# A Mamba layer in two directions: B and C rows, dt and dtx copied together, and dtx made by GpSimd

## The reference, cut to what matters

```python
x = silu(causal_conv(x) + conv_b)                # 256 channels
dt = softplus(x_dbl[..., :64] @ Wdt.T + bdt);  B, C = the 16 + 16 other columns of x @ Wx.T
dA = exp(dt[..., None] * A);  dBx = (dt * x)[..., None] * B[:, :, None, :]
h = dA_t * h + dBx_t;   y_t = sum over 16 states of h * C_t
y = (y + x * Dp) * silu(z);  out = y @ W_out.T
beta = mean(|weight|)                            # of the feed-forward part
w_q = clip(round(weight / (beta + 1e-5)), -1, 1)
```

## Time and profile before

| | |
|---|---|
| median of 3 runs | 1043.89 us (1042.23 to 1044.09) |
| profiled execution | 1041.62 us, span 1039.8 us |
| VectorE (DVE) busy | 906.6 us, 87% |
| GpSimd (POOL) busy | 856.6 us, 82% |
| ScalarE (ACT) busy | 598.6 us, 58% |
| TensorE (PE) busy | 669.3 us, 64% |
| DMA queue q1 | 108.97 MB, 38.1% of 16 engines |

### The profile page before, as it was taken

How to read it: one execution, slowest core, us unless ns; L and a number is a source line. 1 busy time by engine, 2 the same in 40 slices (tenths; PEclk the granted TensorE clock), 3 DMA queues, 4 the chain that set the end, 5 groups by cost and what they waited for, 6 DMA issues and landing times. The chain is left out here.

```text
span 1039.8 us, 9415 instructions
## 1 busy us (share of the span) xinstructions
PE 669.3 (64%) x2124; PEld 221.2 (21%) x2124; DVE 906.6 (87%) x1004; ACT 598.6 (58%) x974; POOL 856.6 (82%) x384
## 2 busy tenths in 40 slices
PE   6537637777667666677567666778576676556432
PEld 3212102222212212122112121213121221012122
DVE  2268769999999999999999999999999999999936
ACT  3436544756476665665476766665575756554414
POOL 0169579999798999999799999997998999997602
PEclk9858867788888788788789889688779788666656
DMA  2344404444343424443453424443433424441002
GB/s 57 99 129 127 143 22 118 140 110 137 95 130 94 130 83 127 133 124 114 114 142 82 137 74 134 127 129 109 120 99 97 142 75 135 124 133 49 0 1 81
DMA packets 84071, 109.56 MB, mean 105 GB/s; under 512 B 21040, under 2 KB 34352, under 8 KB 84016
## 3 DMA queue, kind: packets, MB, share of 16 engines
q1 hardware_dynamic: 84016, 108.97, 38.1%
HBM read 38.65 MB, written 3.15 MB: 40 GB/s over the span
## 5 line engine op out<-in xcount | busy, mean ns | idle before, releaser
L440 POOL TENSOR_TENSOR dbx<-dtx_rep,b_rep 128x1024 f32<-128x1024 f32 x256 | 612.6, 2417 | 63.7 <-DMA dtx_rep<-dtx 45.6
L629 ACT ACTIVATE da_ps<-dt_rep,neg_a 128x512 f32<-128x512 f32 x512 | 350.4, 688 | 339.2 <-DVE hs L892 335.1
L892 DVE TENSOR_TENSOR_SCAN hs<-da_ps,dbx 128x512 f32<-128x512 f32 x256 | 296.9, 1207 | 46.2 <-POOL dbx L440 19.8
L892 DVE TENSOR_TENSOR_SCAN hs<-da_ps,carry,dbx 128x512 f32<-128x512 f32 x256 | 312.2, 1267 | 26.8 <-issue 14.3
L1142 PE MATMUL y_ps<-ch,stack 128*32 128x512 f32 x1024 | 178.4, 775 | 209.7 <-DVE ch L782 135.5
L450 POOL TENSOR_TENSOR ch<-hs,c_rep 128x1024 f32<-128x1024 f32 x96 | 226.1, 2356 | 28.6 <-issue 13.9
L782 DVE TENSOR_TENSOR ch<-hs,c_ps 128x1024 f32<-128x1024 f32 x160 | 191.4, 1196 | 0.0
L1133 PE MATMUL c_ps<-x_dbl,select 128*128 128x512 f32 x256 | 179.5, 789 | 0.0
L1085 PE MATMUL pre<-h_t,w_conv 128*128 128x512 f32 x256 | 120.5, 614 | 7.6 <-ACT xs L530 6.4
L1142 PEld LDWEIGHTS y_ps<-ch,stack 128*32 128x32 f32 x1024 | 24.8, 120 | 324.2 <-issue 220.2
L1133 PEld LDWEIGHTS c_ps<-x_dbl,select 128*128 128x128 f32 x256 | 47.0, 229 | 146.2 <-issue 133.8
(11 more groups left out here) (125 smaller groups left out, 507.7 us busy)
## 6 DMA issues: line engine op xcount, KB each, us to landing
dt_rep<-dt SPq DMA_DIRECT2D x512, 64.0 KB, 2.1
dtx_rep<-dtx SPq DMA_DIRECT2D x512, 64.0 KB, 2.6
b_rep<-bc_rows SPq DMA_DIRECT2D x64, 256.0 KB
c_rep<-bc_rows SPq DMA_DIRECT2D x64, 256.0 KB
h_in<-in_L_attn_hidden_states SPq DMA_DIRECT2D x4, 512.0 KB, 5.6
h_res<-in_L_attn_hidden_states SPq DMA_DIRECT2D x4, 512.0 KB, 6.7
out<-hs SPq DMA_DIRECT2D x4, 512.0 KB, 2.9
bc_rows<-x_dbl SPq DMA_DIRECT2D x16, 64.0 KB, 4.7
```

Source lines behind the costliest of these rows:

```text
L440: nc.gpsimd.tensor_tensor(dbx[:, n % RING], dtx_rep[:, r], b_rep[:, k, :].unsqueeze(1).to_broadcast([P, 2, CHUNK]), ALU.mult).then_inc(dbx ...
L629: nc.scalar.activation(da_ps[:, half % DA_BANKS, :], dt_rep[:, r, e, :], ACT.Exp, scale=neg_a[:, half_of(unit), 2 * (unit % 2) + e, g, k:k ...
L892: nc.vector.tensor_tensor_scan(in_scan_order(hs[:, n % RING, e, :], s), in_scan_order(da_ps[:, (2 * n + e) % DA_BANKS, :], s), in_scan_ord ...
```

## The change

1. dt and dtx become the two halves of one tile `step`, so that one set of 8 copies of 128 KB a slot (`load_step`) replaces `load_dt` and `load_dtx`. Likewise B and C rows lie side by side in HBM and in `bc_rep`, and one load of 512 KB a quad (`load_bc`) replaces `load_b` and `load_c`. Each new load waits for all that either of the old ones waited for.
2. SP's order changes. For the next group: slots 0 and 1, then quads 0, 1 and 2. At a group's start: slots 2 and 3 and quad 3 of the current group.
3. dtx is made by GpSimd (`times_step`), at step 6 instead of 7.
4. GpSimd gives up one C product in kinds 1 and 3 (units 1, 4, 8, 11, 13 instead of 1, 3, 6, 8, 11, 13); VectorE makes it.
5. `w_raw` is loaded early, VectorE sums it right after its first weight copy (line 733), and GpSimd's all-reduce runs before the loop.

```diff
-LATER_STAGES = {"copy x_dbl": 0, "u0": 1, "u1": 2, "take u0": 2, "take u1": 4, "softplus": 5, "dtx": 7}
+LATER_STAGES = {"copy x_dbl": 0, "u0": 1, "u1": 2, "take u0": 2, "take u1": 4, "softplus": 5, "dtx": 6}
...
-POOL_C = ((1, 3, 6, 8, 11, 13),) * NG
+POOL_C = ((1, 3, 6, 8, 11, 13), (1, 4, 8, 11, 13)) * (NG // 2)
...
-        dt = sb("dt", [P, DT, CHUNK])
-        dtx = sb("dtx", [P, DT, CHUNK])
+        step = sb("step", [P, DT, 2, CHUNK])
+        dt, dtx = step[:, :, 0, :], step[:, :, 1, :]
...
+        step_rep = sb("step_rep", [P, 2 * DT, 2, 2, CHUNK])
+        dt_rep, dtx_rep = step_rep[:, :, :, 0, :], step_rep[:, :, :, 1, :]
+        bc_rep = sb("bc_rep", [P, STATES // QUAD, 2, CHUNK])
+        b_rep, c_rep = bc_rep[:, :, 0, :], bc_rep[:, :, 1, :]
...
-        bc_rows = nc.dram_tensor("bc_rows", (NG, 2 * STATES, CHUNK), f32).ap()
+        bc_rows = nc.dram_tensor("bc_rows", (NG, STATES, 2, CHUNK), f32).ap()
...
             load_conv(FWD, conv_in)
+            sp.dma_start(w_raw[:], w_ffn).then_inc(w_raw_in, 16)
...
-                sp.dma_start(bc_rows[s], x_dbl[0:2 * STATES, s % 2, :]).then_inc(rows_stored, 16)
+                sp.dma_start(bc_rows[s].rearrange("n c t -> c n t"), x_dbl[0:2 * STATES, s % 2, :]).then_inc(rows_stored, 16)
+
+            def load_step(b, s, r):
 
                 group = NG * b + s
                 sp.wait_ge(dtx_ready, group + 1)
                 if group:
+                    sp.wait_ge(da_ready, 2 * (UNITS * (group - 1) + last_of_slot(r) + 1))
                     sp.wait_ge(dbx_ready, UNITS * (group - 1) + last_of_slot(r) + 1)
                 for e in range(2):
                     k = BLOCK * (2 * (r % 2) + e)
                     for i in range(QUAD):
+                        sp.dma_start(step_rep[BLOCK * i:BLOCK * (i + 1), r, e], step[k:k + BLOCK, r // 2]).then_inc(step_in[r], 16)
+
+            def load_bc(b, s, k):
 
                 group = NG * b + s
                 sp.wait_ge(rows_stored, 16 * (group + 1))
                 if group:
                     sp.wait_ge(dbx_ready, UNITS * (group - 1) + last_of_quad(k) + 1)
                     sp.wait_ge(ch_pool, pool_c(*before(b, s), last_of_quad(k) + 1))
+                rows = bc_rows[s, QUAD * k:QUAD * (k + 1)].rearrange("n c t -> n (c t)")
+                sp.dma_start(bc_rep[:, k].rearrange("p c t -> p (c t)"),
+                             rows.unsqueeze(1).to_broadcast([QUAD, BLOCK, 2 * CHUNK])).then_inc(bc_in[k], 16)
...
                     if group:
-                        load_dt(b, s, 2)
-                        load_dt(b, s, 3)
-                        load_c(b, s, 3)
+                        load_step(b, s, 2)
+                        load_step(b, s, 3)
+                        load_bc(b, s, 3)
...
                     store_rows(*nxt)
-                    load_dt(*nxt, 0)
-                    load_dt(*nxt, 1)
-                    load_b(*nxt, 0)
-                    load_dtx(*nxt, 0)
-                    load_dtx(*nxt, 1)
-                    load_b(*nxt, 1)
-                    load_c(*nxt, 0)
-                    load_b(*nxt, 2)
-                    load_dtx(*nxt, 2)
-                    load_dtx(*nxt, 3)
-                    load_c(*nxt, 1)
-                    load_b(*nxt, 3)
-                    load_c(*nxt, 2)
+                    load_step(*nxt, 0)
+                    load_step(*nxt, 1)
+                    for k in range(STATES // QUAD - 1):
+                        load_bc(*nxt, k)
 
             store_rows(0, 0)
+            load_bc(0, 0, 0)
+            load_step(0, 0, 0)
+            load_step(0, 0, 1)
             for k in range(1, STATES // QUAD):
+                load_bc(0, 0, k)
             for r in (2, 3):
+                load_step(0, 0, r)
...
+            def times_step(b, s):
+
+                q = NG * b + s
+                pool.wait_ge(dt_ready, q + 1)
+                pool.wait_ge(xs_ready, q + 1)
+                if q:
+                    for k in range(2 * DT):
+                        pool.wait_ge(step_in[k], 2 * QUAD * 16 * q)
+                nc.gpsimd.tensor_tensor(dtx, dt, xs[:, s % 2], ALU.mult).then_inc(dtx_ready, 1)
...
-                        if first and s == 1 and n == 0:
-
-                            pool.wait_ge(w_sum, 1)
-                            nc.gpsimd.partition_all_reduce(tiny[:, 1:2], tiny[:, 0:1], P, REDUCE.add).then_inc(w_sum_all, 1)
...
+                        if n == LATER_STAGES["dtx"] and not (last and s == NG - 1):
+                            times_step(*following(b, s))
...
+            pool.wait_ge(w_sum, 1)
+            nc.gpsimd.partition_all_reduce(tiny[:, 1:2], tiny[:, 0:1], P, REDUCE.add).then_inc(w_sum_all, 1)
+            times_step(0, 0)
...
+            dve.wait_ge(w_raw_in, 16)
+            nc.vector.tensor_reduce(tiny[:, 0:1], w_raw[:], X, ALU.add, apply_absolute_value=True).then_inc(w_sum, 1)
...
-            prepare(0, 0, "dtx")
```

More of the change, by code:

```diff
@@ L215, in build @@
              "rstd_last_ready final_ready stored").split()]
[L218 to L221, removed]
+        bc_in = [sem(f"bc_in{k}") for k in range(STATES // QUAD)]
+        step_in = [sem(f"step_in{r}") for r in range(2 * DT)]
         block = ctx.enter_context(nc.Block())
@@ L317, in store_rows @@
                 sp.wait_ge(x_dbl_sb, NG * b + s + 1)
-                sp.dma_start(bc_rows[s], x_dbl[0:2 * STATES, s % 2, :]).then_inc(rows_stored, 16)
[L320 to L326, removed]
-                    k = BLOCK * (2 * (r % 2) + e)
-                    for i in range(QUAD):
-                        sp.dma_start(dt_rep[BLOCK * i:BLOCK * (i + 1), r, e, :], dt[k:k + BLOCK, r // 2, :]).then_inc(dt_in[r], 16)
-            def load_dtx(b, s, r):
+                sp.dma_start(bc_rows[s].rearrange("n c t -> c n t"), x_dbl[0:2 * STATES, s % 2, :]).then_inc(rows_stored, 16)
+            def load_step(b, s, r):
                 group = NG * b + s
@@ L433, in times_b @@
                 if k == 0:
-                    pool.wait_ge(dtx_in[r], 2 * QUAD * 16 * (group + 1))
+                    pool.wait_ge(step_in[r], 2 * QUAD * 16 * (group + 1))
                 if half_of(n) == 0:
-                    pool.wait_ge(b_in[k], 16 * (group + 1))
+                    pool.wait_ge(bc_in[k], 16 * (group + 1))
                 if not (group == 0 and n < RING):
@@ L445, in times_c @@
                 group, k = NG * b + s, quad_of(n)
-                pool.wait_ge(c_in[k], 16 * (group + 1))
+                pool.wait_ge(bc_in[k], 16 * (group + 1))
                 pool.wait_ge(scanned, 2 * (UNITS * group + n + 1))
@@ L759, in quantise_weight @@
                 nc.vector.tensor_scalar(w_q[:], w_q[:], -1.0, None, ALU.max).then_inc(wq_ready, 1)
-            def prepare(b, s, stage):
-                q = NG * b + s
-                g, c = GROUPS[s]
-                par = s % 2
-                if stage == "dtx":
-                    dve.wait_ge(dt_ready, q + 1)
-                    dve.wait_ge(xs_ready, q + 1)
-                    if q:
-                        for k in range(2 * DT):
-                            dve.wait_ge(dtx_in[k], 2 * QUAD * 16 * q)
-                    nc.vector.tensor_tensor(dtx[:], dt[:], xs[:, par], ALU.mult).then_inc(dtx_ready, 1)
             def times_c(b, s, n):
@@ L918, in batch @@
                             largest(b - 1, 1)
-                        prepares(prepare, b, s, n, last)
                         if first and s == 1 and n == 4:
```

43 lines of the change are left out of this document (7 added, 36 removed).

## The result

The changed kernel takes 1148.59 us (median of 4 runs, 1143.63 to 1149.7) beside 1043.99 for the kernel before: a ratio of 1.0987, with an interval of 1.0942 to 1.1032. The profiled execution took 1149.03 us, its span 1147.1. The forecast was 1044, its range 1018 to 1064: the kernel is 105 us slower than foreseen, far outside.

A forecast was written before the change was run, and what follows sets the result against it. VectorE bounds the kernel before; after the change GpSimd, waiting for quad 3, was to set the pace. The 27 us gained by group 2 are paid back at 7 a batch: 1044 us, range 1018 to 1064.

The forecast's parts named there:

- I take L = 19.2: Steady groups: unit 6's dbx on GpSimd starts 19.2 us after T, the middle of estimates with and without slow copies.
- L: Time from T to the start of GpSimd's dbx of unit 6, which reads quad 3; forecast 19.2 us.
- bound of 20.5: Slower rival: copies hold the four DMA engines as their busy share says, L = 20.5, 1064 us; chance 0.23.
- T: The end of unit 13's C product on GpSimd in each group, from which the prediction counts its times.
- 512 KB take 5.1: Quad 3's load at 101 GB/s: 5.1 us, after 1.4 to its first byte and before 0.6 to the dbx.
- nothing in the way: Rival: copies do not delay quad 3's load, L = 18.0, 1026 us; chance 0.19.
- Their quarter of sixteen 128 KB copies: The 512 KB of copies on the load's four DMA engines ahead of quad 3: 5.1 to 8.2 us.
- T + 1.5 to 6.6: When the four DMA engines were to carry quad 2's load, before their part of the copies and quad 3.
- the prediction's formulas: GpSimd's group period: L + 41.4, L + 37.1, L + 39.4 us in kinds 0 to 2; 60.7 in kind 3.
- each microsecond of L costs 15: Whole kernel: the slower rival's rule that one microsecond more of L, from 19.4 up, adds 15 us.
- quad 3 in time: Rival: the load spreads over all engines, dbx 6 at T + 14.2, VectorE stays the bound, 998 us; chance 0.13.
- then 20 instructions to T: 100.0: Head, group 0: after quad 2 frees dbx 4 at 53.6, 20 GpSimd instructions put T at 100.0 us.

## Why the prediction was wrong, step by step

**The mechanism held in part, and was mis-sized.** Quad 3 behind the C product and behind sixteen copies, GpSimd's wait for it, GpSimd's order setting the pace: all of it is in the trace. What failed is the step "I take L = 19.2", with its bound of 20.5: L is 24.8. The term that failed most is the 5.1 us for a load of 512 KB while copies run beside it. Its terms:
- Quad 3's issue, forecast at T + 10.9, came at T + 11.2 (median). Right.
- "512 KB take 5.1" and the 1.4 and 0.6 around them, 7.1 from issue to dbx. Measured without copy bytes beside it: 7.7 for quad 2, 8.6 for quad 3. One microsecond and a half too short; with this and an issue at T + 11.5 in that kernel, "nothing in the way" was T + 20.2, not T + 18.0.
- "Their quarter of sixteen 128 KB copies", taken from 64 KB copies at a share of 0.41 and 104 GB/s, was put at 5.1 to 8.2 us. Alone, the new copies hold a share of 0.90 while they move 206 GB/s, twice the share for twice the rate. The same working on these gives 57 GB/s on four engines and an estimate of 9.2 us for the quarter, 1 us over the upper bound. The large miss was what stands beside it: from a share of 0.90 almost nothing is left for a load, which takes 0.26 alone. Beside such copies a load needs 13.5 to 13.9 us to its dbx, beside copies of half the size 8.6 to 9.1. I had counted only the copies ahead of a load as in its way, and had the load itself run at its full rate.
- Dbx of unit 4, three products after T, was given no wait, since quad 2 is issued ahead of the copies ("T + 1.5 to 6.6"). It waits 6.6 us, because the copies issued behind it share the engines while it runs. This is the same miss, in the place where I had not looked for it.

The Trainium skill has a rule that I had not weighed (SBUF — State Buffer, "Door 1: The DMA port swizzle"): "DMA bandwidth depends on how many of the 16 SBUF ports your partitions reach". By its mapping a block of 32 partitions in a row reaches 8 of the 16, half of about 435 GB/s, an estimate of 218. The trace agrees, with 206 GB/s for copies of such blocks alone at a share of 0.90. It would have said that 104 GB/s is half of the ceiling and twice that is all of it. No run here has copies of more or other partitions, so that the agreement of this one number is no test of the rule.

**What L cost.** From T to T the periods were 67.7, 62.2, 66.0 and 65.8 us for groups 4 to 7, where the prediction's formulas with these groups' own L (25.0, 23.4, 26.6, 23.9) give 66.4, 60.5, 66.0 and 65.4: the sum over a group was right to 1.7 us. Over the 14 periods from group 0's T to group 14's, L was 25.0 on average, 5.8 over 19.2, which makes 81.5 us; remainders as above make another 10.5. The rest of the miss is the head, group 0's T at 112.1 instead of 100.0 (12.1), and 3.1 after the last of these T: 107.2 in all, the difference between the end of group 15 at 1093.6 and the forecast's 986.4. (By the prediction's own "each microsecond of L costs 15", which counts group 15 too, the median L of 24.8 makes 84.)

**The engines' side was right.** VectorE alone was forecast at 222.9 a batch, with 57.4, 53.6, 50.9 and 61.0 by kind. With the waits gone it is 221.1, with 57.5, 53.3, 50.2 and 60.2. dtx on GpSimd was put at 2.32 and took 2.35, which is 1.9 times VectorE's undisturbed 1.23; dbx fell to 2356 ns, as named. The rival "quad 3 in time", 998 us, is what the kernel with B and C apart does: 999.06. That they meet to 1 us is luck in part: its group 2 starts at 170.7 instead of 160, and what follows takes about as much less than the forecast's terms would have it. What I got wrong was which of the cases this kernel is: the chance of 0.13 lay on a case that came only with B and C apart.

**The head was half right.** The all-reduce is hidden there. GpSimd's timeline of the changed kernel:

```profile
9.94 0.40 POOL L452 PARTITION_ALL_REDUCE tiny<-tiny  x1 [7.83 <-DVE tiny L711]
33.29 2.35 POOL L426 TENSOR_TENSOR step<-step,xs 128x1024 f32<-128x1024 f32 x1 [22.95 <-ACT step L533]
42.51 2.35 POOL L404 TENSOR_TENSOR dbx<-step_rep,bc_rep 128x1024 f32<-128x1024 f32 x1 [6.87 <-DMA step_rep<-step]
...
65.08 2.34 POOL L404 TENSOR_TENSOR dbx<-step_rep,bc_rep 128x1024 f32<-128x1024 f32 x1 [4.59 <-DMA bc_rep<-bc_rows]
```

The hole of group 1 is gone, and alone this is worth 14 us. But dtx began at 33.29 instead of 28.4, for a reason that is not the change's (below), and dbx 4 came at 65.08 instead of 53.6, behind three merged loads and the next sixteen copies. In the kernel with B and C apart dtx starts at 28.78 and dbx 0 at 38.02 (forecast 37.8), so those steps were right; there dbx 8 waits 7.63 us for slots 2 and 3 instead, and group 1 starts at 112.0 all the same. The step "then 20 instructions to T: 100.0" had no wait in it, and each variant has one.

**The parts nearly add up.** Against before: the early all-reduce -14, dtx on GpSimd with the new split of the C products -28, both with the old transfers -38, with the joint copies -44 (ratios 0.9631 and 0.958 of 1044). Merging B and C adds 140 to 150 to either. One part of the change is a loss, and with it the whole came out 10% slower.

**What stays open.** The merged loads were shown to cost the 150 us, and two mechanisms in them: the place in SP's queue behind a C product, and the bytes beside them. Their shares can't be told as one sum, for one grows as the other shrinks (the kernels with 128 KB and with 64 KB copies end at L = 24.8 and 24.9 in different ways). Why quad 3 takes 0.9 us longer than quad 2 with hardly a byte in the copies was not tried; h_res and the store of bc_rows, which run beside it, are the nearest suspects. Whether VectorE or GpSimd is the bound of the kernel of 999.06 us is open too.

## What to carry to other kernels

Before two transfers are joined, list what each has to wait for: the joint one waits for the later of both, and so does all that stands behind it in its queue. A transfer's time alone is no bound when another stream of bytes runs beside it: read the share of the DMA engines for that other stream at its new size, and add the transfer's own; here 0.90 and 0.26 came to more than there is, and the load took nearly twice as long. Where a change has several parts, time them apart; here the joint copies, dtx on GpSimd, the split of the C products and the early all-reduce were together worth 44 us, which the merged loads hid.
